# Four gated cross-attention layers on one core: square sums split in two parts, 96-row heads packed into 128-row tiles, router product widened

## The reference

```
for i in 0..3:
  x = x + tanh(g_xattn[i]) * attention_i(layernorm(x), ctx)
  x = x + tanh(g_ffn[i])   * ffn_i(layernorm(x))
```

```
q = q * rsqrt(mean(q*q) + eps) * q_norm_w      # per token and head
k = k * rsqrt(mean(k*k) + eps) * k_norm_w
probs = softmax(q @ k.T / sqrt(128) + mask);  out = probs @ v;  result = out @ Wo.T
```

## Time and profile before

| | |
|---|---|
| median of 3 runs | 2197.25 us (2195.84 to 2198.91) |
| the profiled execution | 2194.48 us, of which 2192.7 us span |
| PE busy | 1983.3 us (90%) |
| DVE / ACT / POOL busy | 1470.3 (67%) / 1026.8 (47%) / 927.6 us (42%) |
| mean granted TensorE clock | 0.962 |

### The profile page before, as it was taken

One profiled execution on the slowest core, in us unless ns is written; L12 is line 12 of the kernel. 1 busy time (PEld: TensorE's weight loads), 2 busy tenths in 40 slices (PEclk: granted clock), 3 DMA queues, 4 the chain that ended last, 5 costly groups with the idle time before them and its releaser, 6 DMA issues.

```text
span 2192.7 us, 33276 instructions
## 1 busy us (share of the span) xinstructions
PE 1983.3 (90%) x10874; PEld 1660.7 (76%) x10874; DVE 1470.3 (67%) x2725; ACT 1026.8 (47%) x2264; POOL 927.6 (42%) x971
## 2 busy tenths in 40 slices
PE   5999999999747999997997999997889999999998
PEld 4788888887536777776665888886678888888886
DVE  5777777777767777776423555555557766777676
ACT  3666666666414444444112544443145545555542
POOL 2555455544535555455231323322234444444432
PEclk9999999999968999999997999999799999999999
DMA  3212222121310211111110101001101110111001
GB/s 137 64 54 73 87 72 72 47 84 54 97 34 30 78 48 52 48 48 54 48 55 25 33 9 32 17 10 55 53 10 44 44 45 15 44 45 44 16 25 45
DMA packets 47069, 106.77 MB, mean 49 GB/s; under 512 B 6064, under 2 KB 21936, under 8 KB 43104
## 3 DMA queue, kind: packets, MB, share of 16 engines
q1 hardware_dynamic: 46944, 105.14, 15.1%
HBM read 98.37 MB, written 6.75 MB: 48 GB/s over the span
## 4 chain that ended last, share of the span: by engine, by line
PE 64%; DVE 18%; ACT 9%; issue 7%; POOL 1%; ACTq 0%; DVEq 0%; POOLq 0%
PE psX L369 22%; PE psQ L369 13%; PE psS L369 11%; PE psO L369 10%; PE psT L752 5%; DVE pT_lo L906 2%; ACT pT_hi L1083 1%; DVE dq_space L461 1%; PE psT L369 1%; DVE nmax L894 1%; ACT dq_space L448 1%; DVE p_sb L888 1%; DVE nbias L892 1%; ACT oT_hi L1105 1%; ACT p_sb L1076 1%
## 5 line engine op out<-in xcount | busy, mean ns | idle before, releaser
L1191 POOL TENSOR_SCALAR p_sb<-p_sb,rrec 128x512 f32<-128x512 f32 (+1 forms) x320 | 265.9, 831 | 701.7 <-DVE rrec L902 701.6
L1083 ACT ACTIVATE pT_hi<-psT 128x512 fp32r<-128x512 f32 (+2 forms) x384 | 235.0, 612 | 381.4 <-PE psT L752 381.3
L906 DVE TENSOR_TENSOR pT_lo<-psT,pT_hi 128x512 fp32r<-128x512 f32 (+2 forms) x384 | 271.4, 707 | 81.4 <-ACT pT_hi L1083 81.4
L369 PE MATMUL psO<-pT_hi,v_hi 128*128 128x256 f32 (+1 forms) x832 | 255.6, 307 | 70.6 <-DVE oT_lo L927 33.8
L752 PE MATMUL psT<-ident,p_sb 128*128 128x128 f32 x1600 | 242.4, 276 | 13.7 <-POOL p_sb L1191 10.5
L369 PE MATMUL psO<-pT_lo,v_hi 128*128 128x256 f32 (+1 forms) x832 | 237.4, 285 | 0.0
L369 PE MATMUL psO<-pT_hi,v_lo 128*128 128x256 f32 (+1 forms) x832 | 237.3, 285 | 0.0
L752 PEld LDWEIGHTS psT<-ident,p_sb 128*128 128x128 f32 x1600 | 195.0, 142 | 53.1 <-POOL p_sb L1191 15.9
L369 PEld LDWEIGHTS psO<-pT_hi,v_hi 128*128 128x128 f32 (+1 forms) x832 | 155.2, 187 | 85.9 <-issue 40.3
L1076 ACT ACTIVATE p_sb<-psS,nbias 128x512 f32<-128x512 f32 (+1 forms) x192 | 145.3, 757 | 126.5 <-DVE nbias L896 126.5
L369 PE MATMUL psS<-kT_hi,q_hi 128*128 128x512 f32 (+2 forms) x448 | 177.3, 396 | 27.1 <-ACT p_sb L1076 18.7
(11 more groups left out here) (337 smaller groups left out, 4785.3 us busy)
## 6 DMA issues: line engine op xcount, KB each, us to landing
wq_f<-in_a_wq SPq DMA_DIRECT2D x96, 256.0 KB, 2.7
wo_f<-in_a_wo SPq DMA_DIRECT2D x24, 1024.0 KB, 6.8
wkv_f<-in_a_wkv SPq DMA_DIRECT2D x24, 512.0 KB, 4.0
mask_sb<-in_codes SPq DMA_DIRECT2D x32, 174.0 KB, 2.4
qscr<-in_amax SPq DMA_DIRECT2D x32, 174.0 KB, 2.3
w<-qscr SPq DMA_DIRECT2D x32, 174.0 KB, 1.9
wo_f<-in_f_wT SPq DMA_DIRECT2D x3, 1024.0 KB, 4.9
wq_f<-in_a_wq SPq DMA_DIRECT2D x16, 192.0 KB, 2.3
```

Source lines behind the costliest of these rows:

```text
L369: mm = pe.matmul(dst, w, m, start=(first and k == 0), stop=(last and k == n - 1))
L906: L.t_lo.inc(dve.tensor_tensor(pT_view(L, pT_lo, j), t_view(L, j), pT_view(L, pT_hi, j).bitcast(F32), ALU.subtract))
L1083: L.t_hi.inc(act.activation(pT_view(L, pT_hi, j), t_view(L, j), ACT.Copy))
L1191: L.s_norm.inc(pool.tensor_scalar(p_view(L, j), p_view(L, j), rrec[:, j:j + 1], 1.0, ALU.mult, ALU.mult))
```

## The change

1. Fourth layer. The squares are split: ACT writes the square as before, then its rounded part (`qsq_hi`, `ksq_hi`), and POOL the remainder (`q_square_low`, and `k` in POOL's `use`). `column_sums` multiplies both by two columns of ones in fp32r. For `b`, the factor is split on POOL into `k_rhi` and `k_rlo` (two small instructions), two diagonals are written instead of one, and PE makes two fp32r passes. The ones come from a memset on DVE and no longer from a DMA. `q_slot` is (1, 1, 1, 2) instead of (1, 1, 1, 3), and `k0`, `k1` are one slot earlier.
2. Third layer. Query heads 0 to 2 keep rows 0 to 95 of three 128-row tiles, and head 3 is spread over rows 96 to 127 of the three. Query and output products, and the splits of `wq` and `wo`, are 3 to a group instead of 4. ACT and DVE gather head 3's queries by an additional 32-row copy with each tile, and write head 3's output in three copies of 32 rows. The `prep` units are laid out anew.
3. Third feed-forward. The expert and router product has 256 moving columns instead of 136 (the last ones of each product but the last chunk's are the neighbouring chunk's and are not read); its load waits for one more semaphore.

```diff
     dict(kind="plain", hd=96, groups=4, keys=768, slots=4, nbuf=1, ahead=1, settle=1, q_slot=(3, 3, 3, 3),
+         outs=OUT_EARLY, splits=SPLIT_PACKED,
+         prep={(1, 1): ["k0"], (1, 3): ["k1"], (2, 1): ["k2"], (2, 2): ["v0"], (2, 3): ["t0"],
+               (3, 0): ["v1"], (3, 1): ["t1", "v2"], (3, 2): ["t2"]}),
+    dict(kind="rms", hd=128, groups=8, keys=512, slots=4, nbuf=2, ahead=2, settle=2, q_slot=(1, 1, 1, 2),
          outs=OUT_EARLY, splits=SPLIT_TILES,
-         prep={(1, 1): ["k0"], (1, 2): ["k1"], (2, 0): ["k2"], (2, 1): ["v0"], (2, 2): ["t0"],
-               (3, 0): ["v1"], (3, 1): ["t1", "v2"], (3, 2): ["t2"]}),
-    dict(kind="rms", hd=128, groups=8, keys=512, slots=4, nbuf=2, ahead=2, settle=2, q_slot=(1, 1, 1, 3),
-         outs=OUT_EARLY, splits=SPLIT_TILES,
-         prep={(1, 3): ["k0"], (2, 0): ["k1", "m0"], (2, 1): ["m1"], (2, 2): ["b0"], (2, 3): ["v0", "b1"],
+         prep={(1, 2): ["k0"], (1, 3): ["k1"], (2, 0): ["m0"], (2, 1): ["m1"], (2, 2): ["b0"], (2, 3): ["v0", "b1"],
                (3, 0): ["t0"], (3, 1): ["v1"], (3, 2): ["t1"]}),
...
+        def column_sums(pe, dst, hi, lo):
+
+            for m in range(4):
+                to, cols = dst[:, 2 * m:2 * m + 2], slice(m * P, (m + 1) * P)
+                pe.matmul(to, hi[:, cols], ones[:, 0:2], start=True, stop=False)
+                mm = pe.matmul(to, lo[:, cols], ones[:, 0:2], start=False, stop=True)
+            return mm
...
+        def o_parts(L, g, h):
+
+            if h == L.tiles:
+                return [(psO[32 * t:32 * t + 32, :], *(z[L.hd:P, t, :] for z in (oT_hi, oT_lo))) for t in range(L.tiles)]
+            return [(psO[0:L.hd, :], *(oT_view(L, z, g, h)[0:L.hd] for z in (0, 1)))]
...
                 elif kind == "m":
-                    L.k_f.wait(pe, L.count(g, "k", f"k{i}"))
-                    for m in range(4):
-                        mm = pe.matmul(X[:, m:m + 1], ksq[:, i, m * P:(m + 1) * P], ones[:, 0:1],
-                                       start=True, stop=True)
+                    L.k_slo.wait(pe, L.count(g, "k", f"k{i}"))
+                    mm = column_sums(pe, X, ksq_hi[:, i, :], ksq_lo[:, i, :])
                 elif kind == "b":
                     L.k_diag.wait(pe, L.count(g, "b", what))
-                    mm = pe.matmul(X, ones[:, :], diag[:, :, :].rearrange("p a b -> p (a b)"), start=True, stop=True)
+                    pe.matmul(X, ones[:, :], diag_hi, start=True, stop=False)
+                    mm = pe.matmul(X, ones[:, :], diag_lo, start=False, stop=True)
...
             def q_low(g, h):
-                L.q_hi.wait(dve, g.at(4, h + 1))
-                lo, hi, src = q_lo[0:hd, h % 2, :], q_hi[0:hd, h % 2, :].bitcast(F32), psQ[0:hd, :]
+                L.q_hi.wait(dve, g.at(L.tiles, h + 1))
+                hi, lo = q_view(L, g, h)
+                hi, src = hi.bitcast(F32), psQ[0:hd, :]
+                if L.packed:
+                    at = slice(32 * h, 32 * h + 32)
+                    last_hi, last_lo = (z[at] for z in q_last[g.par])
+                    dve.tensor_tensor(last_lo, psQ[hd:P, :], last_hi.bitcast(F32), ALU.subtract)
...
                     if L.rms:
                         L.q_f.inc(act.activation(qscr[:, h % 2, :], psQ[:, :], ACT.Square))
-                        ins = act.activation(dst, psQ[:, :], ACT.Copy, scale=vecs[:, 0:1])
+                        L.q_hi.inc(act.activation(dst, psQ[:, :], ACT.Copy, scale=vecs[:, 0:1]))
+                        L.q_f.wait(act, g.at(4, h + 1))
+                        L.q_shi.inc(act.activation(qsq_hi, qscr[:, h % 2, :], ACT.Copy))
+                        return
...
             def o_high(g, h):
                 L.av_mm.wait(act, g.at(8, 2 * h + 2))
-                L.o_hi.inc(act.activation(oT_view(L, 0, g, h), psO[0:hd, :], ACT.Copy))
+                for src, hi, _ in o_parts(L, g, h):
+                    ins = act.activation(hi, src, ACT.Copy)
+                L.o_hi.inc(ins)
...
+            def q_square_low(g, h):
+                L.q_shi.wait(pool, g.at(4, h + 1))
+                L.q_slo.inc(pool.tensor_tensor(qsq_lo, qscr[:, h % 2, :], qsq_hi.bitcast(F32), ALU.subtract))
...
                     L.k_r.inc(pool.tensor_tensor(k_r[:, i, :], k_ms[:, i, :], half[:, 0:4], ALU.pow))
-                    L.k_r.wait(pool, L.count(g, "m", what))
+                    L.k_r.wait(pool, steps(1))
+                    L.k_r.inc(pool.tensor_tensor(k_rhi[:, :], k_r[:, i, :], ones[:, 0:4].bitcast(F32), ALU.mult))
+                    L.k_r.wait(pool, steps(2))
+                    L.k_r.inc(pool.tensor_tensor(k_rlo[:, :], k_r[:, i, :], k_rhi[:, :].bitcast(F32), ALU.subtract))
+                    L.k_r.wait(pool, steps(3))
                     if i:
                         L.x_mm.wait(pool, L.use(g, "b0")[0] + 1)
-                    L.k_diag.inc(pool.tensor_tensor(diag[:, :, :], ident[:, :].unsqueeze(1).broadcast_to([P, 4, P]),
-                                                    k_r[:, i, :].unsqueeze(2).broadcast_to([P, 4, P]), ALU.mult))
+                    for d, r in ((diag_hi, k_rhi), (diag_lo, k_rlo)):
...
+                    if j == L.q_slot[h] and L.rms and L.head(g, h, L.q_lead):
+                        q_square_low(*L.head(g, h, L.q_lead))
...
-                three(pe, f2_h_banks[t][:, 0:AR], [(xn_tile(t, c), [z[:, c * AR:(c + 1) * AR] for z in (ar_hi, ar_lo)])
+                three(pe, f2_h_banks[t][:, 0:2 * P], [(xn_tile(t, c), [z[:, c * AR:c * AR + 2 * P] for z in (ar_hi, ar_lo)])
                                                    for c in range(DC)]).then_inc(f2_h, 1)
```

More of the change, by code:

```diff
@@ L230, in head, with query, buffer @@
         return to and to[:2]
+    def query(self, g, h, d):
+        to = self.head(g, h, d)
+        return to if to and to[1] < self.tiles else None
+    def buffer(self, g, t):
+        return (self.tiles * g.par + t) % 2
     def slot(self, h, j):
@@ L312, in program @@
         ksq = xn_f
+        with nc.sbuf_tensor("q_even", [P, 2, TOK], F32R) as q_even:
+            pass
         mask_sb = sb("mask_sb", [P, 2 * CTX])
@@ L671, in first @@
                 elif L.i == 3:
[L672 removed]
+                    layers[2].wq_lo.wait(sp, layers[2].tiles * layers[2].n)
                     layers[2].wkv_lo.wait(sp, 2 * layers[2].n)
@@ L716, in q_proj @@
             def q_proj(g, h):
-                L.wq_lo.wait(pe, g.at(4, h + 1))
-                (L.q_f if L.rope else L.q_lo).wait(pe, g.at(4, h) if g.off or g.loop is not None or h else 0)
-                L.q_mm.inc(three(pe, psQ[0:hd, :], [
-                    ([z[:, h % 2, c * hd:(c + 1) * hd] for z in (wq_hi, wq_lo)],
+                L.wq_lo.wait(pe, g.at(L.tiles, h + 1))
+                (L.q_f if L.rope else L.q_lo).wait(pe, g.at(L.tiles, h) if g.off or g.loop is not None or h else 0)
+                n, b = L.wide, L.buffer(g, h)
+                L.q_mm.inc(three(pe, psQ[0:n, :], [
+                    ([z[:, b, c * n:(c + 1) * n] for z in (wq_hi, wq_lo)],
                      (xnT_hi[:, c, :], xnT_lo[:, c, :])) for c in range(DC)]))
@@ L977, in use @@
                 else:
-                    ins = dve.tensor_scalar(q_ms[:, (what[1] + 1) % 2, :], X[:, 0:4], EPS * hd, None, ALU.add)
+                    ins = dve.tensor_scalar(q_ms[:, (what[1] + 1) % 2, :], sums(X), EPS * hd, None, ALU.add)
                 L.x_free.inc(ins)
@@ L1115, in use @@
                     L.k_f.inc(act.activation(ksq[:, i, :], X, ACT.Square))
+                    L.k_f.wait(act, L.count(g, "k", what))
+                    L.k_shi.inc(act.activation(ksq_hi[:, i, :], ksq[:, i, :], ACT.Copy))
                 elif (kind == "k" and L.rope) or kind == "b":
@@ L1156, in head @@
                         o_high(*((g, h - 1) if h else (g.to(-1), 3)))
-                    if j == L.q_slot[h] and L.head(g, h, L.q_lead) and not L.rope:
-                        q_high(*L.head(g, h, L.q_lead))
+                    if j == L.q_slot[h] and L.query(g, h, L.q_lead) and not L.rope:
+                        q_high(*L.query(g, h, L.q_lead))
                     if j == 0 and L.rope and L.head(g, h, 2):
@@ L1204, in use @@
                     L.k_f.inc(pool.tensor_tensor(scr[:, 0, :], scr[:, 0, :], scr[:, 1, :], ALU.add))
+                elif what[0] == "k" and L.rms:
+                    i = int(what[1])
+                    L.k_shi.wait(pool, L.count(g, "k", what))
+                    L.k_slo.inc(pool.tensor_tensor(ksq_lo[:, i, :], ksq[:, i, :], ksq_hi[:, i, :].bitcast(F32),
+                                                   ALU.subtract))
                 elif what[0] == "m":
```

146 lines of the change are left out of this document (91 added, 55 removed).

## The result

The changed kernel takes 2231.0 us (median of 4 runs, 2228.7 to 2233.1) where the kernel before takes 2197.4 beside it: a ratio of 1.0153, 95% interval 1.0135 to 1.0170, some 34 us slower. The forecast was 16 slower, with 2230 as the upper end of the range. The sign was right, the size was half of what came.

The account below looks back on a forecast made before the run. PE's columns were taken as the bound in both layers, savings counting only if other engines' replies arrive in time. Terms -4.5 - 1.4 - 5.6 + 16.1 + 9.2 + 2.5 = +16.3 gave 2213 us, 8-in-10 range 2186 to 2230.

Parts of the forecast that it names:

- 22.2: Fourth attention: forecast of its whole growth in us, from `b`, the border waits, POOL and the prologue.
- -4.5: Third layer: packing saves query and output products, partly lost to waits on copies at group borders; net 4.5 us less.
- -1.4: Router product: the clock rises earlier, so some 7 products at 0.43 take 0.23; 1.4 us less.
- PE stands 2.3 us, at seven borders: +16.1: Fourth layer, slot (0, 0): weighted values wait for `pT_low` behind DVE's queue after the query product moves; 16.1 us more.
- The `b` unit: Fourth layer: two fp32r passes take 0.46 us instead of 0.86, 14 times behind the prologue; 5.6 us less.
- The sums: Fourth layer's square sums: 8 weight loads and 8 short matmuls stay at 0.79 us, following the measured row.
- The copies of 32 rows: Third layer: copies are paid by columns, so 32 rows cost ACT 0.59 and DVE 0.68 us, from 16-row copies.
- rival 3: POOL is worse, small instructions at 1.0 us, and waits long enough to lower the clock: 2229 us; chance 0.12.
- +9.2: Fourth layer: POOL's added work delays the probabilities, 0.8 us at five groups and 2.6 at two loop turns.
- +2.5: Fourth layer's prologue: `m1` waits for its `k_slo` and two diagonals precede the first `b`; 2.5 us more.
- -2.0 for the end products: Third layer's end: PE needs 4 x 0.69 less, but DVE's layer norm statistics become the limit; 2.0 us less.
- Rival 2: Fourth layer's replies are covered altogether, decided at slot (0, 0) by `pT_low`; kernel faster at 2185 us; chance 0.18.

Follow-up runs that it names:

- e3: Only the fourth layer's change, third layer and router product as in the kernel before: 2223.1 us, ratio 1.0115.
- e1: Only the third layer's packing, router product and fourth layer as in the kernel before: 2198.6 us, ratio 1.0005.
- e2: The kernel before with only the router product widened to 256 columns: 2195.7 us, ratio 1.0000.
- e8: The changed kernel run again, unaltered, beside the kernel before: 2234.4 us, ratio 1.0158.
- e5: Fourth layer's change alone, plus sixteen unread products filling PE's wait ahead of the weighted values in slot (0, 0): 2218.2 us, ratio 1.0088.
- e6: Fourth layer's change alone, with unit `t1` in slot (3, 3) instead of (3, 2): 2209.6 us, ratio 1.0055.
- e12: Third layer's packing alone, plus 28 extra products filling the wait before the end products: 2198.4 us, ratio 1.0005.
- e4: Fourth layer's change alone, with the query product back in slot (3, 3): 2203.4 us, ratio 1.0033.
- e10: Fourth layer's change alone with query product in (3, 3), and the last two `wo` remainders later on POOL: 2216.6 us, ratio 1.0081.
- e11: Kernel before with `b` in two passes, `k0`, `k1` earlier, the 256-column router product and fourteen fill products behind it: 2193.7 us, ratio 0.9978.
- e7: Kernel before with only `b` in two fp32r passes and `k0`, `k1` one slot earlier: 2193.5 us, ratio 0.9984.
- e9: Third layer's packing alone, with two of three copies of head 3's output left out (output incomplete): 2190.6 us, ratio 0.9964.

## Why the prediction was wrong

**The balance.** Against the median before, the forecast was 15.7 us slower, and 33.6 came: 18 too little. The parts alone account for 10 of them: the fourth layer +25 (e3) for 22.2, the third +1.1 (e1) for -4.5, the router 0.0 (e2) for -1.4. That the fourth layer's sum came so near is luck: it left out 9.6 for the clock, and had some 5 too much for POOL and the prologue. The other 7 to 8 came only with the parts together, and the intervals of the runs allow chance; they stay open.

**What held.** The queue on DVE at slot (0, 0), "PE stands 2.3 us, at seven borders: +16.1": 2.27 and 15.9, in the order of instructions that it listed. The `b` unit, 0.86 to 0.46. The sums, left at the length they had: 0.81 before and after, with two columns for one. The Trainium skill's figure for a load and matmul pair at 128 columns (TensorE: Matmul & The Clock Gate, "Back-to-back issue gap") is some 81 ns. The rows after have 0.11 us between such products of two columns at full clock, so to go by the row was right. The copies of 32 rows, 0.59 and 0.69. In the router stage, that PE is not sooner through, since it waits for `wo_lo`.

**The step that failed first: "PE stands 2.3 us, at seven borders: +16.1".** It prices the wait by its length alone. Behind it the clock fell, in after's profile at three borders, in e8's at six, and each fall costs 2.9 to 3.6 us more (e3 against e5): 9.6 in a profile with three. In the fourth layer, clock falls had a place only in rival 3, as following from POOL; in the third they were in the upper bound alone. e5 removes the falls and keeps `pT_low` late, and the 9.6 go from the attention; e6 shortens the waits to 1.35 and the falls at the borders go too. This is shown. Why it is three in one execution and six in another is not. The Trainium skill says (same page, "A second HAM failure mode: psum-queue depth-cycling") that short idle times between groups of matmuls can be enough to make the clock swing, and (under "What's actually happening") that when it changes level differs between runs of one kernel. The rows agree with both: seven equal waits of 2.27, three falls in one execution and six in another.

**POOL, "+9.2".** The waits for POOL and `q_ms` in the stretch are 8.3 after (4.7 + 3.6) and 3.2 before: +5.1. The small instructions took 0.204 each where I took 0.35, so a group had 0.6 less on POOL, and PE waits 0.58 a group where 0.8 stood, and 2.6 and 2.8 at the two turns of the loop where 4.1 stood. (The scaling row of 0.373 under the earlier trace rows, from which the 0.35 was taken, lies in the second layer and not in the fourth attention.) Mis-sized by 4, to the other side.

**Prologue, "+2.5":** +1.4. Fourth attention in all: -5.6 + 15.9 + 9.6 + 5.1 + 1.4 = 26.4 of 28.7. Most of the last 2.3 is in how a wait is counted: a record is longer than the distance to the next, so the 2.27 of idle time stand for more. From the border's transposes to the weighted values it is 2.87 at each of the seven borders, where transposes took 0.35 before, and that is 2.52 a border, 1.8 more in all.

**Third layer, "-4.5".** The borders: PE loses 0.97 + 1.80 where before it lost nothing. A middle group took 82.7 instead of 84.1, -1.4 where -1.9 was forecast: right in kind and near in size. The end was not: from the last group's start to the router product 103.1 instead of 96.5, with a forecast of about +1. 2.6 of it is the wait before the end products (1.45 to 4.04), as forecast; 2.0 is the clock behind it (e12); and some 2 are no part of the change, for the unchanged third layer takes 377.0 to 377.2 in e2, e3, e4, e5, e6, e10 and e11 and 374.9 in e7: before's profile with 374.7 lacked a stretch at half clock that most have. The forecast's -2.0 for the end products is the term that failed: from that wait to the router product it was 15.2 us before, 14.9 in after, and 12.8 in e12, where the clock is up. By timing, the packing is worth +1.1 us (-1.5 to +3.5), and e9 shows that its content is real and that the copies eat it: two copies less on each of two engines, and the layer is 10.1 shorter.

**Router, "-1.4".** The product does go faster at the upper clock level: granted 0.50 under it in the earlier trace rows, 0.82 in after, where the clock rose 2.4 us into it, and 1.00 in e2, where it was up from the start. Its width costs next to nothing, as forecast: 0.12 a product for 0.11 at full clock. But "that some 7 products at 0.43 would take 0.23" left out what the wait for `wo_lo` does: PE stands idle for 3.4 us, and the clock falls behind that wait again. In after's trace the base product came to 13.9 us; in time the part is worth 0.0 (e2).

**Rivals.** Rival 3 had the time (2229) by luck: POOL was better than forecast, and the clock fell behind waits for DVE. Rival 2's point of decision, `pT_low` 8 us after the start of (3, 2), was right, as e4 shows from the other side: with the query product in (3, 3) the border costs 0.8.

## What to carry to other kernels

A wait that recurs on TensorE is to be priced twice: its length, and the chance that the clock falls behind it; here waits of 2.27 us at the borders brought three or six falls in seven, and waits of 1.35 in the same place none. The length alone does not decide: in the last group, where PE has less work between its waits, a wait of 1.43 brought a fall in 4 of 14 profiles. Where an instruction is moved up to spare a wait behind it, count what the move takes from the cover of the next one: 5.3 us of waits were bought off for 15.9. And take a change of several parts apart before judging it: `b` in two passes alone is 0.2% faster than the kernel before, and the rest of the change more than ate it.

## What the chip showed beyond the forecast

- The clock falls that a 2.27 us wait brings are not the same from execution to execution of one kernel (three and six of seven), and those in e3 cost 2.9 to 3.6 us each; products into a bank that is overwritten anyway, at 0.12 us each, prevent them (e5).
- A plain POOL instruction on 4 columns takes 0.204 us, a power on 4 columns 1.017, a diagonal of 512 columns 1.042, a remainder of 512 columns 1.29.
- The router product's 48 products of 256 columns stand 0.12 us apart at full clock (e2), those of 136 columns 0.11 (e12), and both 0.21 at half clock (after). The wider product was the quicker one only because the clock rose under it.
